# Attention scores from two fp32r parts, two heads on the two halves of the partitions, and row maxima of 2 or 4 heads in one instruction

## The chip, the cores and the metric

The kernel runs on one core of a Trainium2 chip. The metric is the device time of one execution in microseconds (us). Engines: PE multiplies matrices (PEld loads its weights), DVE is VectorE, ACT is ScalarE, POOL is GpSimd, SP issues most of the transfers.

## The reference

One block of a transformer on x of shape (2, 1024, 256), fp32, with 16 heads of 16:

```python
h = _layernorm(x) * (1 + ca) + sa                  # from silu(c) @ wmod
q, k, v = split(h @ W_qkv.T + b_qkv)               # 16 heads of 16
scores = einsum('bnqd,bnkd->bnqk', q, k) * 16 ** -0.5
attn = softmax(where(causal, -inf, scores))        # over keys
x = x + ga * (out @ W_out.T + b_out)
h = _layernorm(x) * (1 + cb) + sb
x = x + gb * ffn(h)      # router over 16 experts (4 groups, top 2; top 4 experts), shared expert
```

The gates and the router's choice of experts need attention's output close to fp32, which is why q and k go through several products.

## The kernel before

**Before attention.** Tokens come in four chunks of 512. For each, DVE makes the statistics (`first_statistics`, L1476), ACT the root, PE turns the rows (`turn`), ACT evicts them as high part and DVE or POOL make the low part, and PE projects q and k in four tiles (`M_ORDER`; L2085) and v (L2107). The bias is added by ACT twice: as fp32 (L1291) and rounded to bf16 (L1294). The tile is then split in three bf16 parts: for chunks 0 and 1 by DVE (`split_tile`: L1540, L1542, L1544), for chunks 2 and 3 by POOL, ACT, POOL (L1063, L1278, L1068). The three parts of q and k are written to DRAM (`qk_parts`, L795) in six rows for each feature, by `Q_PARTS` and `K_PARTS`, so that one product over 6 x 16 = 96 rows gives the sum of six products of parts. `stage` (L797) reads them back, 96 partitions for one group of four heads, in three slots.

**Attention** is a loop over 8 iterations (2 batches x 4 groups of 4 heads). In each, 12 steps (`STEPS`: query half, key tile) have four scores, one for each head (`scores`, L2157; keys x up to 512 queries, causal parts left out). ACT takes the exponential of each out of PSUM (L1377), POOL masks diagonal tiles (L1217), and PE multiplies with the values (`products`, L2140, fp32, a head to each 32 columns of the array). The maximum of each row is taken off inside the product: three more rows of q hold it in three bf16 parts, against ones in k, so that a score is a product over 99 rows. These maxima come from a second set of scores, the units (`score_unit`, L2054; queries x up to 512 keys), which PE makes for iteration n + 1 while it works on n: 48 units for each iteration, one head each, 32 of them with a product that adds the causal mask (L2060). DVE reduces each with one instruction (`row_maximum`, L1511, L1517). `max_parts` (L1605) splits the negated maxima, PE turns them (L2130), `max_copy` brings them to SBUF and `aug` (L725) writes them with three transfers into q's rows 96 to 98.

**Order.** Each engine works its instructions in order. `interleave` (L118) writes PE's order: a score, then as many units as their cost asks for, and after each fourth score the value products of the step before. Units use three banks of PSUM in turn (0 to 2), scores three (3 to 5), products bank 6, the transposes of outputs and maxima bank 7. A score waits for the exponential three before it, a unit for the reduction three before it. In iterations 4 to 6 DVE, PE and ACT also carry pieces of the output projection and of the router (`UNIT_DVE`, `LATE_PE`, `LATE_ACT`); iteration 7 has no units. In chunk 3's projections PE issues 36 of the units of iteration 0 between the other matmuls, 3 (`PER`) at a time, and the last 12 after them. SP's queue holds the writes of parts, the stages, the values and most of the small transfers of the maxima.

**After attention** come the shared expert, the routed blocks of 128 rows (79) and the sums.

## Time and profile before

| | us |
|---|---|
| median of 3 runs | 651.16 (649.86 to 651.72) |
| span of the profiled execution | 644.6 |
| around the span (median less span) | 6.6 |
| before attention | 0 to 89.3 |
| attention, 8 iterations | 89.3 to 369.7 |
| shared expert, routing, sending | 369.7 to 460 |
| routed blocks, sums | 460 to 644.6 |
| busy: PE, DVE, ACT, POOL | 582.1 (90%), 487.5 (76%), 382.8 (59%), 337.9 (52%) |

The execution's own time stands for its span and the 6.6 us around it. Busy times are sums over the whole span; what an engine's saving is worth depends on who is late in each stretch. The ends of matmuls are modelled, so for PE the distance from one start to the next says more than the duration. "fp32r" tiles show as f32 in the rows of matmuls.

### The profile page before, as it was taken

The numbers are of one execution on the slowest core, as the hardware profiler recorded it, in microseconds if no ns is written. First come the engines' busy times: TensorE is split into PE (matmuls) and PEld (weight loads), VectorE is DVE, ScalarE is ACT, GpSimd is POOL, SyncE is SP. The second block draws the span as 40 slices with busy tenths as digits, with TensorE's granted clock in tenths as the row PEclk, the third lists the DMA queues.
The fourth block names the chain that finished last, engine by engine and source line by source line (L and its number), as shares of the span: only waits on it lengthen the run. The fifth ranks groups of instructions, "written<-read, shape, count | busy, mean of one in ns | idle before, by whom it ended". The sixth has DMA issues, their size and how long they took to land. (4 is left out here: it accounts for less than half of the span.)

```text
span 644.6 us, 13664 instructions
## 1 busy us (share of the span) xinstructions
PE 582.1 (90%) x3960; PEld 395.7 (61%) x3960; DVE 487.5 (76%) x1415; ACT 382.8 (59%) x926; POOL 337.9 (52%) x585
## 2 busy tenths in 40 slices
PE   3879879999999999998997799997799999999996
PEld 3657533434343444444342378776799999999985
DVE  4888978888888868776967568898566766666648
ACT  3546437666766656655858552643356777776662
POOL 5524614455747527763738876774144444444430
PEclk9989969999999999998999989999799999999999
DMA  8349965961707273451305243665964444444498
GB/s 270 137 158 288 334 221 151 243 210 71 216 26 224 87 209 141 136 185 63 118 34 174 77 150 115 232 217 207 364 220 134 135 135 134 133 135 134 126 374 335
DMA packets 69066, 113.62 MB, mean 176 GB/s; under 512 B 12578, under 2 KB 51106, under 8 KB 67844
## 3 DMA queue, kind: packets, MB, share of 16 engines
q1 hardware_dynamic: 62036, 93.74, 45.3%
q0 software_dynamic: 6864, 19.01, 7.6%
q8 instruction: 34, 0.56, 0.4%
q14 instruction: 36, 0.29, 0.1%
q10 hardware_dynamic: 96, 0.01, 0.0%
HBM read 60.57 MB, written 49.94 MB: 171 GB/s over the span
## 5 line engine op out<-in xcount | busy, mean ns | idle before, releaser
L1377 ACT ACTIVATE Pr<-bank 128x512 f32<-128x512 f32 (+3 forms) x384 | 165.5, 494 | 94.8 <-PE bank L2166 91.1
L1517 DVE TENSOR_REDUCE mxA<-bank 128x1 f32<-128x128 f32 (+3 forms) x256 | 112.2, 484 | 23.9 <-PE bank L2062 23.7
L1233 POOL DMA_INDIRECT expert_rows<-Y,YIX x79 | 75.7, 959 | 104.0 <-DVE ytmp L1938 75.5
L2166 PE MATMUL bank<-Qs,Ks 99*128 99x512 bf16 (+3 forms) x384 | 118.6, 332 | 8.0 <-ACT Pr L1377 3.8
L2062 PE MATMUL bank<-Ks,Qs 96*128 96x512 bf16 (+3 forms) x384 | 122.1, 334 | 2.2 <-DVE mxA L1517 1.3
L1517 DVE TENSOR_REDUCE mxB<-bank 128x1 f32<-128x512 f32 x128 | 81.5, 681 | 13.5 <-PE bank L2062 13.4
L2152 PE MATMUL bank<-Pr,Vst 128*32 128x512 f32 (+3 forms) x768 | 83.4, 507 | 4.4 <-POOL Pr L1217 4.4
L1167 POOL DMA_INDIRECT chosen_rows<-Hx,pos x64 | 69.9, 1093 | 21.1 <-issue 17.5
L2415 PE MATMUL bank<-W,xh 128*128 x316 | 78.3, 329 | 0.4 <-issue 0.4
L1215 POOL TENSOR_TENSOR tick<-ident 128x1 f32<-128x1 f32 x128 | 25.4, 198 | 100.5 <-ACT Pr L1377 99.7
L2166 PEld LDWEIGHTS bank<-Qs,Ks 99*128 99x128 bf16 x384 | 36.0, 98 | 61.4 <-ACT Pr L1377 38.7
L2060 PE MATMUL bank<-mask,identb 128*128 128x128 bf16 x256 | 55.1, 227 | 7.7 <-DVE mxA L1517 5.3
L1968 DVE TENSOR_TENSOR act_a<-bank,sg 128x176 f32<-128x176 f32 x79 | 27.0, 342 | 45.3 <-ACT sg L1424 45.2
L2062 PEld LDWEIGHTS bank<-Ks,Qs 96*128 96x128 bf16 x384 | 38.1, 99 | 28.8 <-DVE mxA L1517 6.1
L1217 POOL TENSOR_SCALAR_AFFINE_SELECT Pr<-Pr 128x256 f32<-128x256 f32 x128 | 53.3, 416 | 0.0
L2415 PEld LDWEIGHTS bank<-W,xh 128*128 128x128 f32 x316 | 52.3, 189 | 1.3 <-issue 1.0
L2415 PE MATMUL bank<-W,xl 128*128 x158 | 51.3, 325 | 0.0
L1424 ACT ACTIVATE sg<-bank 128x176 f32<-128x176 f32 x79 | 25.1, 317 | 37.4 <-PE bank L2415 37.4
L2060 PEld LDWEIGHTS bank<-mask,identb 128*128 128x128 bf16 x256 | 25.1, 98 | 30.0 <-DVE mxA L1517 13.6
L1439 ACT ACTIVATE Y<-bank 128x256 f32<-128x256 f32 x79 | 30.3, 384 | 13.7 <-PE bank L2444 5.4
L1931 DVE TENSOR_TENSOR xl<-bank,xh 128x256 fp32r<-128x256 f32 x79 | 32.9, 416 | 5.8 <-ACT xh L1418 5.8
L2369 PE MATMUL bank<-ident,G 128*128 128x128 f32 x158 | 30.9, 278 | 6.0 <-DMA G<-chosen_rows 6.0
(254 smaller groups left out, 1314.8 us busy)
## 6 DMA issues: line engine op xcount, KB each, us to landing
G<-chosen_rows SPq DMA_DIRECT2D x79, 132.0 KB
Z<-expert_rows SPq DMA_DIRECT2D x16, 512.0 KB, 12.3
W<-expert_words SPq DMA_DIRECT2D x7, 1088.0 KB, 7.1
qk_parts<-AP SPq DMA_DIRECT2D x16, 384.0 KB, 5.0
Qs<-qk_parts SPq DMA_DIRECT2D x16, 384.0 KB, 4.2
Ks<-qk_parts SPq DMA_DIRECT2D x8, 768.0 KB, 9.0
Wraw<-in_wexp SPq DMA_DIRECT2D x9, 608.0 KB, 5.1
SA<-in_wexp SPq DMA_DIRECT2D x7, 608.0 KB, 10.5
```

The source lines that it names most:

```text
L1167: nc.gpsimd.indirect_dma_start(out=xd, out_offset=bass.IndirectOffsetOnAxis(ap=pos[:, c * TPC + t, j:j + 1], axis=0), in_=chosen(c)[:, t, ...
L1217: nc.gpsimd.affine_select(out=v, in_=v, compare_op=ALU.is_ge, fill=0.0, base=0, pattern=[[0, 2], [1, P]], channel_multiplier=-1).then_inc( ...
L1233: nc.gpsimd.indirect_dma_start(out=zd, out_offset=bass.IndirectOffsetOnAxis(ap=YIX[:, b:b + 1], axis=0), in_=Y[b % YRING], in_offset=None) ...
L1377: nc.scalar.activation(Pr[(2 * s + j // 2) % 4][:, j % 2, 0:w], ebank[p % RING][:, 0:w], ACT.Exp, scale=SCALE).then_inc(exp_done, EXP)
L1517: nc.vector.tensor_reduce(dst, mbank[u % RING][:, 0:w], AX.X, ALU.max).then_inc(m_red, 1)
L1931: nc.vector.tensor_tensor(xl[u % 2][:, :], xbank[:, 0:H], xh[u % 2][:, :].bitcast(F32), ALU.subtract).then_inc(xl_done, 1)
L2060: nc.tensor.matmul(mbank[u % RING][:, w - P:w], identb[:, :], mask[:, :], start=True, stop=False, skip_group_check=True)
L2062: nc.tensor.matmul(mbank[u % RING][:, 0:w], Qs[slot][0:NPR, i // TPC, j, (i % TPC) * P:(i % TPC + 1) * P], Ks[slot][0:NPR, j, k0:k0 + w], ...
L2152: ins = nc.tensor.matmul(pvb[32 * j:32 * j + 32, q0:CH], Vst[slot][:, kt, 32 * j:32 * j + 32], Pr[(2 * s + j // 2) % 4][:, j % 2, 0:w], st ...
L2166: nc.tensor.matmul(ebank[p % RING][:, 0:CH - q0], Ks[slot][0:NAUG, j, kt * P:(kt + 1) * P], Qs[slot][0:NAUG, qc, j, q0:CH], start=True, st ...
L2369: ins = nc.tensor.transpose(xbank[:, k * P:(k + 1) * P], G[u % GRING][:, k * P:(k + 1) * P], ident[:, :])
L2415: ins = nc.tensor.matmul(ubank[u % 2][:, 0:2 * EI], x_part[u % 2][:, k * P:(k + 1) * P], words(u, first + k * 2 * EI, 2 * EI), start=(k == ...
```

## The change

- q and k are split in two parts, kept in fp32 words that TensorE reads as fp32r, and three products of parts (high x high, low x high, high x low) stand in 48 rows in place of six in 96. The splitting: ACT writes the high part (one instruction for chunks 0 and 1, two for 2 and 3), and one DVE or POOL instruction writes the low part; DVE reads the bank itself.
- Two heads stand in one tile, on partitions 0 to 47 and 64 to 111 (`SIDES` = 2, `PAIRS` = 2). The maxima take two rows in place of three, so that a score is a product over 50 rows. `stage` has six transfers in place of three, `aug` four in place of three, writes of a tile two in place of three. Bytes are the same.
- A unit is one or two pairs of heads: 4 heads where 2 pairs x width fit a bank (widths 128 and 256), else 2. It has two banks, one for each side, and one DVE instruction reduces all of it. There are 20 units an iteration, in two slots of two banks (0 to 3). Through the same slots go the transposes of maxima and outputs and the late pieces (up to the last iteration). Scores use banks 4 to 6, products 7.
- The mask is added for each side in two products with 64 rows each, with a table and its copy with swapped halves.
- In chunk 3, 12 units stand between the projections, one (`PER`) at a time.
- The ones in k are written by small transfers in place of POOL's memsets; one zero fill of the block tiles moves to DVE behind attention.

```diff
-Q_PARTS = (0, 1, 2, 0, 1, 0)
-K_PARTS = (0, 0, 0, 1, 1, 2)
+Q_PARTS = (0, 1, 0)
+K_PARTS = (0, 0, 1)
 NPR = len(Q_PARTS) * HD
-NAUG = NPR + 3
+NMAX = 2
+NAUG = NPR + NMAX
+SIDES = 2
+PAIRS = HG // SIDES
+SIDE = P // SIDES
+UNIT_LIST, ROW_FIRST, ROW_COUNT = [], [], []
+for _row in ROWS:
+    _groups = [(0, PAIRS)] if PAIRS * _row[3] <= CH else [(a, 1) for a in range(PAIRS)]
+    ROW_FIRST.append(len(UNIT_LIST))
+    ROW_COUNT.append(len(_groups))
+    UNIT_LIST += [_row + group for group in _groups]
-UNITS = len(ROWS) * HG
+UNITS = len(UNIT_LIST)
...
-    unit_cost = [w + 200 for _, _, _, w in ROWS for _ in range(HG)]
+    unit_cost = [n * SIDES * (w + 100) for _, _, _, w, _, n in UNIT_LIST]
-        while u < UNITS and units * sum(head_cost) < heads * sum(unit_cost):
+        while p % SIDES == SIDES - 1 and u < UNITS and units * sum(head_cost) < heads * sum(unit_cost):
...
-PER = 3
+PER = 1
...
-        mbank, ebank, pvb, tb = allb[0:RING], allb[RING:2 * RING], allb[6], allb[7]
+        mbank = [banks[:, 2 * s:2 * s + 2, :] for s in range(2)]
+        ebank, pvb = allb[4:4 + RING], allb[7]
...
+            for part in range(NMAX):
+                for l in range(SIDES):
+                    row, first = SIDE * l + NPR + part, (part * SIDES + l) * PAIRS * TPC
+                    queue.dma_start(
+                        Qs[slot][row:row + 1, half, :, :].bitcast(F32).rearrange("o a (i q) -> o (a i) q", i=TPC),
+                        MT[half][first:first + PAIRS * TPC, :]
+                    ).then_inc(aug_in[slot][half], 16)
...
-                nc.vector.tensor_tensor(Rq[i % 2][:, :], Fq[m], PT[c % 2][:, 0, m, :], ALU.subtract).then_inc(split_step, 1)
-                dve.wait_ge(split_step, 2 * k + 1)
-                nc.vector.tensor_copy(PT[c % 2][:, 1, m, :], Rq[i % 2][:, :]).then_inc(split_step, 1)
-                dve.wait_ge(split_step, 2 * k + 2)
-                nc.vector.tensor_tensor(PT[c % 2][:, 2, m, :], Rq[i % 2][:, :], PT[c % 2][:, 1, m, :],
-                                        ALU.subtract).then_inc(parts_done[0], 1)
+                tile = PT[k % 8]
+                dve.wait_ge(qk_read, k + 1)
+                nc.vector.scalar_tensor_tensor(out=tile[:, 1, :].bitcast(F32R), in0=qkbank[k % QK_RING], scalar=Bqk[:, m:m + 1],
+                                               in1=tile[:, 0, :], op0=ALU.add, op1=ALU.subtract).then_inc(parts_done[0], 1)
...
-                dst = mxA[:, i, j:j + 1] if diag else mxB[:, i - TPC, j:j + 1]
-                nc.vector.tensor_reduce(dst, mbank[u % RING][:, 0:w], AX.X, ALU.max).then_inc(m_red, 1)
+                dst = (mxA[:, :, i] if diag else mxB[:, :, i - TPC]).rearrange("p (l a) -> p a l", l=SIDES)[:, first:first + pairs]
+                src = mbank[USE[piece][0]][:, :, 0:pairs * w].rearrange("p l (a w) -> p a l w", a=pairs)
+                if pairs == 1:
+                    dst, src = dst[:, 0], src[:, 0]
+                nc.vector.tensor_reduce(dst, src, AX.X, ALU.max).then_inc(read_of(piece), 1)
...
                 if diag:
-                    nc.tensor.matmul(mbank[u % RING][:, w - P:w], identb[:, :], mask[:, :], start=True, stop=False,
-                                     skip_group_check=True)
-                nc.tensor.matmul(mbank[u % RING][:, 0:w], Qs[slot][0:NPR, i // TPC, j, (i % TPC) * P:(i % TPC + 1) * P],
-                                 Ks[slot][0:NPR, j, k0:k0 + w], start=not diag, stop=True,
-                                 skip_group_check=True).then_inc(m_ps, 1)
+                    for part in range(2):
+                        for l in range(SIDES):
+                            rows, k = slice(SIDE * l, SIDE * (l + 1)), P if part == 0 else SIDE
+                            table = (plain, swapped)[part ^ l]
+                            to = bank[:, l, 0:pairs * w].rearrange("p (a w) -> p a w", a=pairs)[:, :, w - k:w]
+                            nc.tensor.matmul(to, table[rows, 0, :],
+                                             table[rows, 1:2, P - k:P].broadcast_to([SIDE, pairs, k]), start=part == 0, stop=False,
+                                             skip_group_check=True)
+                for a in range(first, first + pairs):
+                    for l in range(SIDES):
+                        rows = slice(SIDE * l, SIDE * l + NPR)
+                        ins = nc.tensor.matmul(bank[:, l, (a - first) * w:(a - first + 1) * w],
+                                               Qs[slot][rows, i // TPC, a, (i % TPC) * P:(i % TPC + 1) * P],
+                                               Ks[slot][rows, a, k0:k0 + w], start=not diag, stop=True, skip_group_check=True)
+                ins.then_inc(m_ps, 1)
...
+                a, l = j // SIDES, j % SIDES
+                rows = slice(SIDE * l, SIDE * l + NAUG)
+                nc.tensor.matmul(ebank[p % RING][:, 0:CH - q0], Ks[slot][rows, a, kt * P:(kt + 1) * P],
+                                 Qs[slot][rows, qc, a, q0:CH], start=True, stop=True).then_inc(e_ps, 1)
```

## Rows read from the trace of the kernel before

**Rows 1.** Busy us of each engine (instructions), granted clock, DMA share, GB/s, by stretch
```profile
121.00:152.80 31.80, 31.08 (x238) 12.83 (x235) 27.07 (x64) 21.62 (x50) 18.61 (x48) 1.00 0.63 190
217.20:257.00 39.80, 37.21 (x275) 17.47 (x272) 31.24 (x82) 23.56 (x54) 19.47 (x56) 1.00 0.44 142
335.50:369.70 34.20, 27.73 (x186) 10.78 (x185) 21.24 (x67) 25.52 (x61) 27.95 (x51) 1.00 0.35 118
340.00:360.00 20.00, 16.53 (x115) 6.72 (x115) 13.44 (x45) 15.81 (x35) 16.37 (x26) 1.00 0.49 164
360.00:380.00 20.00, 15.68 (x97) 9.11 (x95) 12.87 (x26) 10.43 (x23) 16.78 (x29) 0.83 0.23 85
```

**Rows 2.** Waits in iteration 1: total us, times, longest
```profile
ACT Pr L1377 <- PE bank L2166: 10.0, 12, 1.3
PEld bank L2166 <- ACT Pr L1377: 4.5, 7, 0.8
DVE mxA L1517 <- PE bank L2062: 1.9, 6, 0.4
```

**Rows 3.** Timeline of PE, a step of iteration 5: start, duration
```profile
273.28 0.38 PE L2062 MATMUL bank<-Ks,Qs 96*128 96x512 bf16 x1
273.59 1.06 PE L2152 MATMUL bank<-Pr,Vst 128*32 128x512 f32 x8
274.58 0.39 PE L2166 MATMUL bank<-Qs,Ks 99*128 99x512 bf16 x1
...
275.42 0.38 PE L2166 MATMUL bank<-Qs,Ks 99*128 99x512 bf16 x1
275.64 0.22 PE L2060 MATMUL bank<-mask,identb 128*128 128x128 bf16 x1
275.70 0.27 PE L2062 MATMUL bank<-Ks,Qs 96*128 96x256 bf16 x1
275.81 0.38 PE L2166 MATMUL bank<-Qs,Ks 99*128 99x512 bf16 x1
```

**Rows 4.** Timeline of PE, the transposes of an output
```profile
286.36 0.66 PE L2137 MATMUL bank<-ident,OT 128*128 128x128 f32 x4
286.86 0.33 PE L2166 MATMUL bank<-Qs,Ks 99*128 99x384 bf16 x1
```

**Rows 5.** Timeline of PE in chunk 2's projections, and two lines' instructions (min/median/max ns)
```profile
54.95 0.39 PE L2085 MATMUL bank<-hh,Wqkh 128*128 128x512 f32 x1
55.18 0.39 PE L2085 MATMUL bank<-hl,Wqkh 128*128 128x512 f32 x1
...
56.11 0.28 PE L2107 MATMUL bank<-Wvh,hl 128*128 128x256 f32 x1
56.23 0.28 PE L2107 MATMUL bank<-Wvl,hh 128*128 128x256 f32 x1
...
L2085 PEld LDWEIGHTS bank<-hl,Wqkh x32: 187/190/334, 18.3 to 69.8; 128*128 128x128 f32 x32
...
L2062 PEld LDWEIGHTS bank<-Ks,Qs x384: 95/98/152, 60.5 to 334.9; 96*128 96x128 bf16 x192
```

**Rows 6.** Timeline of DVE in iteration 1
```profile
130.58 0.20 DVE L1619 TENSOR_SCALAR MP<-mxA 128x16 bf16<-128x16 f32 x1
...
131.37 0.17 DVE L1626 TENSOR_TENSOR MP<-mr,MP 128x16 bf16<-128x16 f32 x1
...
132.09 2.47 DVE L1517 TENSOR_REDUCE mxB<-bank 128x1 f32<-128x512 f32 x4
134.49 0.95 DVE L1517 TENSOR_REDUCE mxA<-bank 128x1 f32<-128x128 f32 x4
```

**Rows 7.** Timelines of DVE, ACT and PE before attention, with idle time and releaser
```profile
30.62 0.68 DVE L1540 TENSOR_TENSOR Rq<-Pr,AP 128x512 f32<-128x512 f32 x1
31.33 0.43 DVE L1542 CAST AP<-Rq 128x512 bf16<-128x512 f32 x1
31.80 0.69 DVE L1544 TENSOR_TENSOR AP<-Rq,AP 128x512 bf16<-128x512 f32 x1
...
40.95 0.21 ACT L1251 ACTIVATE rstd<-rvar 128x4 f32<-128x4 f32 x1 [11.05 <-DVE rvar L1490]
...
42.36 0.80 PE L2085 MATMUL bank<-hh,Wqkh 128*128 128x512 f32 x1 [4.42 <-ACT AP L1294]
```

**Rows 8.** Busy times with DMA share and GB/s, and PE's first score
```profile
75.00:80.00 5.00, 3.82 (x23) 1.89 (x21) 5.00 (x13) 0.00 (x0) 0.43 (x1) 1.00 1.09 383
...
89.32 0.59 PE L2166 MATMUL bank<-Qs,Ks 99*128 99x512 bf16 x1 [3.01 <-DMA Qs<-MT]
```

343 lines of the change are left out of this document (185 added, 158 removed).

## The prediction

> **What bounds the kernel now.** I first read the busy times by stretch [rows 1]. The span of the profiled execution is 644.6 us, and the sum below is made against it. The median of the runs is 651.16 us, 6.6 us more, which lies around the span and which nothing here touches. Attention takes 280 of the 644.6 us, from 89.3 to 369.7. A plain iteration (0 to 3) takes 31.8 us, in which PE is busy for 31.1, DVE 27.1 and ACT 21.6. Iterations 4 to 6, which also carry the output projection and the router, take 38.6 to 39.9 us; 4 is shown. Iteration 7 has no row maxima and takes 34.2 us, with PE at 27.7. Before attention, maxima of iteration 0 are made under the projections and after them.
>
> The waits of iteration 1 [rows 2] say who is late: ACT waits 10.0 us for scores of PE, PE's weight loads wait 4.5 us for ACT, DVE waits 1.9 us. So PE is ahead of nobody: it sets the pace. The busy time of PE is modelled, so I checked it with starts in the timeline [rows 3]. A 512-wide bf16 score takes 0.22 us from start to start, a 256-wide one 0.11, a 128-wide mask product 0.06. The four value products of a step take 0.99 us, in which fp32 needs four passes: 4 x 0.22 = 0.88 for all four heads, so the four column groups already run at the same time. That leaves 0.11 behind them, and the matmul ahead of them takes 0.31 in place of 0.22, so a step pays 0.2 for going to column groups and back.
>
> The sum for PE in a plain iteration: scores 24 x 0.22 + 8 x 0.17 + 8 x 0.11 + 8 x 0.06 = 8.0 us (the widths between by proportion); maxima units the same, 8.0; masks 32 x 0.06 = 1.9; products 9 full-width steps' worth x 0.88 + 12 x 0.20 = 10.3; two transposes of outputs at 0.50 [rows 4] and two of maxima at about 0.2, 1.4. Together 29.6 of 31.8: 2.2 us are stalls. PE is the bound of the loop, and DVE is next.
>
> **Scores and maxima.** Parts fall from six bf16 products over 96 rows to three fp32r ones over 48. Two heads stand on partitions 0 to 63 and 64 to 127, so two successive matmuls use separate halves of the array's rows and write separate banks. No row shows two row halves at once; the column groups of [rows 3] show the like, and I take the same for rows. The price of a single fp32r matmul is in the projections [rows 5]: 512 wide 0.23 us, 256 wide 0.12, each with a weight load of its own that lasts 0.19 against 0.098 in bf16. So one load of fp32r weights passes at least every 0.12 us. I price a pair at 0.24: two loads, with the columns (0.23) under them. The 24 pairs of maxima take 5.8 us and the 24 of scores 5.8, against 8.0 each. Widths under 256 are not shown in fp32r; between 0.06 (bf16) and 0.12 (the load), a pair costs at most the 0.24 that I take, unless the narrow form is much slower.
>
> Masks: each of 12 diagonal units now has four products (two halves of the table on two sides), 48 x 0.06 = 2.9 against 1.9, +1.0. A pair of them could share 0.06, so the lower bound is 1.4. The transposes of maxima and outputs use all rows and stand between products and scores, one more change of shape for each of four, 4 x 0.1 = 0.4. PE's sum becomes 5.8 + 5.8 + 2.9 + 10.3 + 1.4 + 0.4 = 26.6, 3.0 less.
>
> On this the Trainium skill (TensorEngine Tiling, Key Properties) says that changing the tiling mode, not just the tile, drains the engine. The 0.31 and the 0.11 behind 0.88 in [rows 3] agree with it. It also speaks against the change in chunk 3, where 12 units in row halves stand between full-array projections: at 0.1 for each of 24 changes that would be 2.4 us on PE, and with all of it exposed the forecast would be 623 in place of 621.
>
> **DVE.** Four 512-wide reductions in a row take 2.47 us and four 128-wide 0.95 [rows 6]. Less the tail of the last (0.08), that is 0.60 and 0.22 each, so 1.0 ns a column and 0.09 fixed. The columns (18,432 an iteration) stay; 20 instructions do what 48 did, which saves 28 x 0.09 = 2.5 us (0 if reading two banks with one instruction costs as much as it spares). The parts of the maxima lose two of four steps at 0.2 each [rows 6], twice an iteration: 0.8. DVE falls from 27.1 to 23.8 and is not the end: it still has waits for PE's transposes. ACT keeps 21.6. The extra row-maximum buffers are two slots of two banks, which hold 2 x 1.1 us of reductions where three banks held 3 x 0.6, so products of 0.99 are still covered. But maxima and output transposes now pass through the same two slots, and their copies (0.2 and 0.7 us) stand in that ring. With the engines so close I don't let the stalls vanish: 26.6 + 2.2 = 28.8 if all stay, 26.6 if none; DVE's lead grows by 3.3 - 3.0, so its share of the stalls stays and a part of the waits for ACT, whose ring of three now gets scores sooner, goes: I take 28.3. **Saved: 3.5 us** an iteration, in 0 to 3: 14. In 4 to 6 the same scores and units pass under the same PE bound (37.2 busy of 39.8 in 4), 3.5 x 3 = 10.5. In 7 no units run and ACT's own work and waits fill it: 0.
>
> **Before attention.** In the first chunk DVE splits four tiles at 1.8 us each (three instructions) [rows 7]; behind them in its queue stand the statistics of chunk 3, for which ACT waits 11.05 us, and ACT's queue holds the evictions for which PE waits 4.42. One instruction of 0.69 at most replaces the three: 4 x 1.15 = 4.6 us, all on that chain. The second chunk's split lies beside a dense PE. From 73 us on DVE's maxima bound; they save another 2.5 + 0.8 once. Against it stand the transfers: [rows 8] has the DMA engines full at 383 GB/s, and the first score at 89.32 waits 3.01 us for the rows of maxima that had to pass them. The bytes are the same (six of 2 against three of 4), so this stage ends no sooner than its start was moved. SP has eight small transfers more ahead of the first write, at a time in which it is idle (its last load is issued at 11 us, the first write at 25.7). ACT's four small issues in place of three (+0.6) lie under the last reductions. I take 5.5, between 4 and 7. Behind attention only banks and one memset move: 0.
>
> **The sum.** 651.2 - 14 - 10.5 - 5.5 = 621.2, predicted **621** (span about 614.6).
>
> **The rivals.**
> The row halves do not overlap (the change doesn't do what it says). Each fp32r matmul then costs 0.23, 0.175, 0.12 and 0.12: 17.7 for both kinds against 16.0, masks 3.3 against 1.9, transposes +0.1, so +3.2 an iteration: 651.2 + 7 x 3.2 - 5.5 + 1 = **669**, slower. The place is every pair of scores and units; it decides where less than about half of the overlap comes, since 29.6 lies midway between 26.6 and 32.8. The column groups speak against it, and the missing row for it.
> They overlap in part. At 0.30 a pair in place of 0.24, 48 pairs cost 2.9 more; where 512 wide only, 24 x 0.06 = 1.4 an iteration, 10 in all: **631**. The Trainium skill (TensorE: Matmul & The Clock Gate, Measured speedup vs the span model) has four row tiles at 3.07 times; an estimate by it is 77% of the ideal, which gives this 0.30.
> PE's lighter load lets its clock fall. From 340 to 360 us it is granted 1.00 with PE busy for 16.5 of 20, from 360 to 380 only 0.83 with 15.7 [rows 1]. At 1.2 GHz for a tenth of the loop, 2.6 us an iteration: **639**. It was at 1.00 through all plain iterations, and steps leave no long idle piece.
> Both relieved fully: two halves load weights at the same time, masks pair at 1.4, and stalls shrink as queues are looser: PE 24, DVE 23.8, an iteration of 26: 651.2 - 7 x 5.8 - 7 = **604**.
>
> **How the numbers follow.** Forecast 0.55, full relief 0.08, partial 0.14, clock 0.05, no overlap 0.13; 0.05 is left for what I don't see, 0.03 of it near no change and 0.01 on either side. A measurement of this kernel tells 0.3% from no change. Faster is 0.55 + 0.08 + 0.14 + 0.05 + 0.01 = 0.83, same 0.03, slower 0.14. The likeliest's own range is 612 to 630 (unknown stalls of 1 us an iteration either way). The range 603 to 650 leaves out no overlap and half of full relief, under 2 in 10.
>
> **What would show it.** In the timeline two scores or two units of different sides start within 0.05 us of each other where both banks are free; apart by 0.23, the last rival holds. A plain iteration takes about 28.3 us, with ACT's wait for PE well under 10 us. A four-head reduction of 256 wide takes 1.1 to 1.2 us. Iteration 7 stays at 34. ACT's wait for the statistics falls from 11 to about 6 us, and the first score starts near 84. The prediction is wrong if the two slots make PE wait for DVE, if narrow fp32r matmuls are far slower than their loads, or if the sharing of slots by the transposes holds back the maxima.

## The result, and the profile after

The changed kernel takes 708.25 us (median of 4, 704.25 to 710.82) against 650.51 us for the kernel before on the same chip (649.14 to 651.72): a ratio of 1.088, 95% interval 1.084 to 1.092. Here and below, times are medians of a kernel's fast runs (within 1.5% of its fastest), and the profiles of e1 and e5 are of slower runs. It is 58 us slower where 30 us faster were forecast. The profiled execution took 709.61 us with a span of 706.9, against a span of 644.6.

The page after, cut to the busy line and TensorE's granted clock in 40 slices of 17.7 us:

```profile
PE 629.8 (89%) x4088; PEld 432.5 (61%) x4088; DVE 460.1 (65%) x1144; ACT 373.3 (53%) x910; POOL 324.5 (46%) x565
...
PEclk9999658995699659989669578999979999999999
```

DVE and ACT are no busier than before (487.5 and 382.8 us there), PE is, by 48 us, though its parts fell from six to three. The digits 5 and 6 in the clock line say that in a good part of attention PE had its lower clock, 1.2 GHz (0.50).

The same in stretches: the first is attention from 76 us to the last copy of outputs (L1364), the second what lies behind; the third and fourth are two passes through the same steps, from the copy of one half of outputs to the next, at either clock. Columns are busy us and instructions of each engine, granted clock, DMA share, GB/s.

```profile
76.00:433.90 357.90, 315.93 (x2061) 152.27 (x2062) 216.60 (x355) 183.09 (x423) 170.61 (x410) 0.78 0.41 119
433.90:706.90 273.00, 255.72 (x1704) 236.10 (x1704) 193.48 (x678) 159.54 (x439) 129.25 (x130) 0.97 0.57 194
...
128.10:138.50 10.40, 9.21 (x85) 4.77 (x85) 8.25 (x13) 6.37 (x18) 6.74 (x17) 1.00 0.53 121
167.70:183.90 16.20, 15.69 (x85) 8.01 (x85) 8.18 (x12) 6.69 (x17) 9.03 (x20) 0.50 0.46 88
```

The same view of the kernel before, the matching stretches:

```profile
76.00:373.90 297.90, 271.58 (x1950) 116.52 (x1949) 235.08 (x596) 184.03 (x422) 169.11 (x411) 0.97 0.46 146
373.90:644.60 270.70, 253.65 (x1704) 234.84 (x1704) 193.16 (x677) 159.31 (x439) 129.25 (x130) 0.98 0.57 195
...
124.36:133.64 9.28, 9.18 (x74) 4.09 (x73) 7.86 (x19) 6.40 (x18) 5.70 (x16) 1.00 0.58 133
124.36:156.16 31.80, 31.07 (x235) 12.83 (x234) 27.07 (x64) 21.61 (x52) 18.61 (x46) 1.00 0.52 154
```

(The third row is this half of an iteration, the fourth a whole iteration.)

Since the clock has two levels, a mean of 0.78 over 357.9 us means 2 x 0.22 x 357.9 = 157 us at 1.2 GHz; before, 0.03 x 2 x 297.9 = 18 us. (The mean has two decimals, so such a figure is good to some 4 us.) The same 85 products take 16.2 us at the low clock and 10.4 at the high one, so each microsecond at the low clock loses 5.8 / 16.2 = 0.36. By that rate, an estimate from one pair of stretches, **the clock costs (157 - 18) x 0.36 = 50 us.** The span grew by 62.3 us. The first score comes 3.3 us earlier, what lies behind attention takes 2.3 us more, so attention from its first score grew by 63.3, and 13 us of this remain. At the high clock too the changed kernel is the slower one, 10.4 against 9.3 us in this half of an iteration. Two pauses add 5.8 us: PE waits 2.86 us at 155.69 and 2.94 us at 235.50 for GpSimd's masks, and in the kernel before no wait of this kind is over 1 us until 371 us. Two different things failed, then: a large one, the clock, and a saving that isn't there at either clock.

The waits from 100 to 400 us, to be set beside [rows 2] (which are for one iteration):

```profile
ACT Pr L1435 <- PE bank L2245: 139.7, 84, 5.2
...
DVE mxA L1578 <- PE bank L2126: 67.0, 49, 6.0
PEld bank L2245 <- ACT Pr L1435: 57.5, 99, 1.7
```

Everyone waits for PE's products, and PE's loads wait for ACT; no wait for DVE's slots or the turned maxima is among the large ones.

The timeline of a pair of scores and a pair of maxima at the full clock answers to [rows 3]:

```profile
215.11 0.66 PE L2213 MATMUL bank<-ident,OT 128*128 128x128 f32 x4
215.69 0.50 PE L2245 MATMUL bank<-Qs,Ks 50*128 50x512 f32 x2
216.03 0.39 PE L2126 MATMUL bank<-Ks,Qs 48*128 48x512 f32 x2
216.26 0.39 PE L2245 MATMUL bank<-Qs,Ks 50*128 50x512 f32 x1
216.92 0.49 PE L2245 MATMUL bank<-Qs,Ks 50*128 50x512 f32 x1 [0.28 <-ACT Pr L1435]
```

Two halves start as one (x2), so they do overlap. But the pair at 215.69 is followed only 0.34 us later, the next pair 0.23 us later. The first stands behind transposes over all rows, with no wait of PE before it. Then one score of the next pair starts alone, since the bank of the other isn't free yet (it waits 0.28 us for ACT): the halves are out of step.

The reductions over two banks in the groups by shape:

```profile
L1578 DVE TENSOR_REDUCE mxB<-bank 128x2 f32<-128x1024 f32 x64 | 78.2, 1223 | 29.5 <-PE bank L2126 28.5
```

PE's timeline has the first score, as in [rows 8]:

```profile
86.00 0.80 PE L2245 MATMUL bank<-Qs,Ks 50*128 50x512 f32 x2 [2.25 <-DMA Qs<-MT]
```

### The profile page after: what moved, and what is told of

Same layout as the page of the kernel before. It is cut to its first block and busy times, and to the rows that moved or that the text cites. A ratio compares the mean times of both kernels' runs of the same rounds, so it can differ in the third digit from the quotient of the medians.

```text
span 706.9 us, 13625 instructions
## 1 busy us (share of the span) xinstructions
PE 629.8 (89%) x4088; PEld 432.5 (61%) x4088; DVE 460.1 (65%) x1144; ACT 373.3 (53%) x910; POOL 324.5 (46%) x565
## 5 line engine op out<-in xcount | busy, mean ns | idle before, releaser
L1578 DVE TENSOR_REDUCE mxA<-bank 128x4 f32<-128x512 f32 (+2 forms) x96 | 99.3, 1046 | 76.4 <-PE bank L2126 75.6
L2245 PE MATMUL bank<-Qs,Ks 50*128 50x512 f32 (+3 forms) x384 | 126.0, 492 | 22.2 <-ACT Pr L1435 18.8
L2245 PEld LDWEIGHTS bank<-Qs,Ks 50*128 50x128 f32 x384 | 60.5, 223 | 101.2 <-ACT Pr L1435 68.3
L2229 PE MATMUL bank<-Pr,Vst 128*32 128x512 f32 (+3 forms) x768 | 102.8, 616 | 8.5 <-POOL Pr L1284 8.5
L2126 PE MATMUL bank<-Ks,Qs 48*128 48x512 f32 (+3 forms) x384 | 104.6, 470 | 3.0 <-DVE mxA L1578 1.0
L1578 DVE TENSOR_REDUCE mxB<-bank 128x2 f32<-128x1024 f32 x64 | 78.2, 1223 | 29.5 <-PE bank L2126 28.5
L2126 PEld LDWEIGHTS bank<-Ks,Qs 48*128 48x128 f32 x384 | 55.5, 235 | 8.1 <-DVE mxA L1578 2.3
L2120 PE MATMUL bank<-plain 64*128 64x128 bf16 (+1 forms) x192 | 38.8, 255 | 7.5 <-DVE X L1705 1.9
L2229 PEld LDWEIGHTS bank<-Pr,Vst 128*32 128x32 f32 x768 | 16.6, 119 | 36.1 <-issue 14.4
L2120 PE MATMUL bank<-swapped 64*128 64x128 bf16 (+2 forms) x192 | 38.2, 257 | 0.0
L1982 DVE TENSOR_TENSOR xl<-bank,xh 128x256 fp32r<-128x256 f32 x79 | 32.8, 415 | 6.1 <-ACT xh L1476 6.0
```

The source lines that it names most:

```text
L1578: nc.vector.tensor_reduce(dst, src, AX.X, ALU.max).then_inc(read_of(piece), 1)
L1982: nc.vector.tensor_tensor(xl[u % 2][:, :], xbank[:, 0:H], xh[u % 2][:, :].bitcast(F32), ALU.subtract).then_inc(xl_done, 1)
L2120: nc.tensor.matmul(to, table[rows, 0, :], table[rows, 1:2, P - k:P].broadcast_to([SIDE, pairs, k]), start=part == 0, stop=False, skip_grou ...
L2126: ins = nc.tensor.matmul(bank[:, l, (a - first) * w:(a - first + 1) * w], Qs[slot][rows, i // TPC, a, (i % TPC) * P:(i % TPC + 1) * P], Ks ...
L2229: ins = nc.tensor.matmul(pvb[32 * j:32 * j + 32, q0:CH], Vst[slot][:, kt, 32 * j:32 * j + 32], Pr[(2 * s + j // 2) % 4][:, j % 2, 0:w], st ...
L2245: nc.tensor.matmul(ebank[p % RING][:, 0:CH - q0], Ks[slot][rows, a, kt * P:(kt + 1) * P], Qs[slot][rows, qc, a, q0:CH], start=True, stop=T ...
```

## The experiments

Thirteen kernels. Times of the kernel before are from the same chip and occasion. "Low" is the time at 1.2 GHz between 76 us and the last copy of outputs, worked out from the stretch's mean clock as above.

**Is a stacked pair as cheap as thought?** Two kernels of TensorE series alone: all series run warm, then again behind a pause of about 11 us, with full-array bf16 products after each. Core of the first:

```python
S1 = [("halves","r",50,512), ("halves","b",50,512), ("halves","r",64,512), ("full","b",99,512),
      ("full","r",99,512), ("one","r",50,512), ("full","b",50,512)]   # halves: rows 0.. and 64.. in turn
```

> A kernel of its own: it computes nothing of the reference (the input is copied to the output) and issues 512-wide matmuls on random data in series: fp32r on 50 rows of alternate halves, bf16 on 50 rows of alternate halves, fp32r on 64 rows of alternate halves, bf16 on 99 rows, fp32r on 99 rows, fp32r on 50 rows of one half, bf16 on 50 rows alone; each series runs 96 or 72 matmuls, pauses about 10 us, runs as many again, and full-array bf16 stands between series. Each matmul has its own weights. Theory A, the fp32r weight load holds up the pair: a pair of halves costs 0.34 us in fp32r and about 0.22 in bf16. Theory B, row halves overlap only partly: 0.34 in both types. Theory C, the clock does not come back on half-used rows: after the pause the 50-row series stay at granted 0.50 to their end (over 20 us), while the 99-row ones are back at 1.00 within 7 us. Rival D, pauses alone set the clock: all series come back within 7 us.

> The same kernel of its own with narrow matmuls: fp32r on 50 rows of alternate halves 256 and 128 wide, bf16 on 64 rows of alternate halves 128 wide, fp32r on 99 rows 128 wide, fp32r on 128 rows 256 wide. If the load of fp32r weights sets the pace, 256 and 128 wide cost the same in halves, 0.12 us a matmul or more. If narrow fp32r is slow in itself, the 128-wide one on 99 rows takes over 0.12 us. Clock: by theory C the series in halves stay at 0.50 after the pause, by rival D they come back.

The fp32r halves of 50 rows in turn, then (behind "...") the same product on one half only, each in a stretch without a pause:

```profile
48.50:59.30 10.80, 10.80 (x97) 9.18 (x96) 0.00 (x0) 0.00 (x0) 1.00 0.00 0
...
334.00:364.00 30.00, 30.00 (x71) 23.02 (x72) 0.00 (x0) 0.00 (x0) 0.50 0.00 0
```

In the second: halves of 256 columns, of 128, of 128 again behind a pause, and one product of 99 rows and 128 columns after another, at first and later:

```profile
49.30:55.00 5.70, 5.70 (x95) 5.70 (x96) 0.00 (x0) 0.00 (x0) 1.00 0.00 0
85.10:90.40 5.30, 5.30 (x97) 5.30 (x96) 0.00 (x0) 0.00 (x0) 1.00 0.00 0
103.00:111.00 8.00, 8.00 (x78) 8.00 (x78) 0.00 (x0) 0.00 (x0) 0.50 0.01 2
...
153.80:160.40 6.60, 6.60 (x61) 6.57 (x59) 0.00 (x0) 0.00 (x0) 1.00 0.01 2
180.00:199.00 19.00, 19.00 (x91) 19.00 (x91) 0.00 (x0) 0.00 (x0) 0.50 0.00 1
```

In a stream a pair costs 0.23 us for 512 columns (10.8 / 97 is 0.11 a product), so neither the loads nor a partial overlap hold it up: both theories fall. At the full clock 256 columns cost 0.06 us a half and 128 hardly less, 0.055 (96 products in 5.3 us); alone, 99 rows of 128 columns cost 0.11. Of the clock, neither theory C nor rival D holds as it stood. Halves in turn, 512 wide, kept 1.00 and had it back in their second series behind the pause, against theory C. But one half alone fell to 0.50 in the middle of its first series, with no pause before, and sat there with PE busy all the time, 0.42 us a product, and so did 99 rows of fp32r 128 wide; halves 128 wide ran at 0.50 behind the pause to the end of their series. That speaks against rival D.

**Few rows inside the kernel.** The kernel before, with three of its six bf16 products left out (51 and 48 rows, one head after the other):

```diff
-Q_PARTS = (0, 1, 2, 0, 1, 0)
-K_PARTS = (0, 0, 0, 1, 1, 2)
+Q_PARTS = (0, 1, 0)
+K_PARTS = (0, 0, 1)
```

> The kernel before with three bf16 products of two parts in place of six of three: products over 48 and 51 rows, one head after the other, nothing stacked, all else as before; the third part of q and k and the products with it are left out of the scores. Theory C, few rows in use keep the clock down: PE's work is the same in columns, but the clock stays at 0.50 for long pieces of attention and the time is above 680 us. Rival D, the pauses and the stacking do it: the clock is as before, and the time is 640 to 651 us, since a third of the written rows is gone from the start.

835.97 us in the fastest run (three others took 853.03 to 857.58) against 659.31 (656.5 to 663.22), 27% slower, with as many products of the same widths, and less data. Its attention, in the run of 853.03:

```profile
76.00:573.40 497.40, 484.28 (x1967) 149.11 (x1967) 257.24 (x601) 199.19 (x423) 172.17 (x413) 0.57 0.23 70
```

2 x 0.43 x 497.4 = 428 us low, of 497. Beside the rows in use only the bytes of staging and a few early writes changed, so this shows the mechanism in the kernel itself: with half the rows in each product and the same number and widths of products, the clock was low for 86% of this stretch.

**More rows, pairs in step, fillers.** Four edits of the changed kernel.

```diff
 e2: scores over both halves (zeros in the unused rows between)
-                rows = slice(SIDE * l, SIDE * l + NAUG)
+                rows = slice(0, SIDE + NAUG)
 e3: one wait for a pair
-                if n or p >= RING:
-                    pe.wait_ge(exp_done, n * (EXP * HEADS) + EXP * (p - RING + 1))
+                if p % SIDES == 0 and (n or p + 1 >= RING):
+                    pe.wait_ge(exp_done, n * (EXP * HEADS) + EXP * (p + 1 - RING + 1))
 e4: a product of all rows ahead of each unit of maxima; e5: e3 and e4
+                nc.tensor.matmul(bank[:, 0, 0:4 * P]..., identb, plain[:, 1:2, :].broadcast_to([P, 4, P]),
+                                 start=True, stop=True, skip_group_check=True)
```

> The changed kernel, with each score product run over rows 0 to 113 of its two tiles, so over both halves at once, in place of its own 50 rows; rows 32 to 63 are set to 0 in the beginning so that the unused ones add nothing. What it computes is the sum of the two stacked heads' scores for either of them: each head's own scores are left out. The number and width of the products stay the same, but two of them can no longer run beside each other. Clock theory (products that use half of the array's rows let the clock fall, and keep it at 1.2 GHz): the 50-row products are now those of the row maxima alone, the scores at 229 ns each keep the clock up for most of the attention; the low stretches, some 165 us up to 440, shrink to under 80, mean granted clock 0.93 or more, and the time falls by 30 to 60 us, to 650 to 680. Out-of-step theory (the pair of halves doesn't overlap because its second score waits for an exponential, and the halves lag): there was little overlap to lose, and none is won: 700 to 725, the clock as it was at 0.88.

> The changed kernel with one wait moved: the first score of a stacked pair waits until the banks of both are free, and the second for nothing, so that the two issue together and run beside each other. Nothing is left out. Out-of-step theory: a pair at full clock goes from 0.34 to 0.24 us (512 wide); 24 pairs an iteration, some 1.5 to 2.5 us of each of 8 iterations, and as the PE has to wait less at a low clock also a few more: 680 to 695. Clock theory: the pair is shorter and the engine idles more, still with half of the rows, so the low stretches stay (160 us or more up to 440) or grow, and the time stays within 1% of 708 or goes up.

> The changed kernel with one product over 128 rows and 512 columns (bf16, constant tables) in front of each unit of the row maxima, into the unit's own bank, which the unit then starts anew. Nothing is left out. It adds 160 products of 0.216 us at full clock: 34.6 us of TensorE time, 4.3 an iteration. Clock theory: products of all rows between those of half the rows keep the clock up or bring it back; the low stretches shrink to under 80 us up to 440 and the time falls by 10 to 40 us in spite of the added work, to 670 to 700. Out-of-step theory: only work is added, on an engine that was busy 89%: 730 to 745. If the clock follows pauses alone (rows have no part), it is the same as the latter at 0.88.

> Both edits of the two kernels before this one together: pairs of scores in step, and a product of all rows in front of each unit. Nothing is left out. Clock theory with full overlap: 34.6 us of added products, 20 us saved by pairs, the clock at 1.00 for most of the attention: 640 to 675. Out-of-step theory alone: the fillers' 35 us against 20 saved: 715 to 725. Neither: as the one with fillers alone.

Against 649.52 us (647.07 to 651.92) before: e2 711.93 (706.72 to 714.22), ratio 1.095; e3 697.3 (693.31 and 701.31), 1.074; e4 728.5 (727.26 and 729.74), 1.122; e5 726.4 (721.78 and 731.06), 1.120. e3 to e5 have two runs each. Attention in e2, e3 and e4, and in e2 a whole iteration at full clock:

```profile
76.00:436.00 360.00, 329.48 (x2111) 156.77 (x2110) 224.89 (x365) 187.83 (x425) 176.28 (x413) 0.85 0.43 128
...
178.09:212.23 34.14, 33.19 (x251) 15.34 (x252) 24.65 (x32) 21.76 (x51) 18.78 (x46) 1.00 0.44 115
```

```profile
76.00:428.60 352.60, 296.65 (x2061) 131.14 (x2062) 217.31 (x355) 186.82 (x423) 172.03 (x410) 0.78 0.41 121
```

```profile
76.00:452.00 376.00, 346.47 (x2217) 148.90 (x2216) 222.08 (x359) 185.06 (x423) 170.82 (x410) 0.86 0.38 112
```

Low time: 157 us in the changed kernel, 108 in e2, 155 in e3, 105 in e4. Rows do lift the clock, as the clock theory says, but its forecasts of the time missed. In e2, 49 us less at the low clock are worth 18 us by the rate above. Its zeros are written first, so that its first copy of outputs comes 9 us later than in the changed kernel (112.4 us against 103.2); from there to the last copy it takes 323.6 us against 330.7, 7 us less, and running the scores one after the other ate the rest. In e4, 52 us less at the low clock are worth 19 us, the fillers are 35 us of work, and the time is 20 us above the changed kernel's. What I expected of e2 and e4 took the clock for the whole loss. e5 missed the 640 to 675 us of the clock theory too. Its time is 2 us under e4's, which is nothing, given the spread, so it is as the one with fillers alone; its profile is of a run of 743.89 us and isn't compared.

Out-of-step, the rival, missed as well: e3 lies between the two forecasts for it, some 10 us under the changed kernel. e3 did put the pairs in step and took 19 us off PE's busy time in attention. But halves of an iteration with the same clock in both kernels got no shorter: 10.7 us against 10.4 at full clock, and 16.2 and 18.2 us at 0.50 in either. The gain stands in one place. From the copy of outputs at 218 or 219 us to the one two halves later, e3 takes 37.2 us and the changed kernel 46.9, because one of the pauses for GpSimd is missing and only 7 us are low there in place of 27. The half at full clock says why pairs in step save nothing, e3 here, the changed kernel above:

```profile
129.20:139.90 10.70, 8.79 (x87) 4.25 (x85) 8.43 (x12) 6.52 (x19) 6.87 (x17) 1.00 0.61 136
```

PE is busy 0.4 us less and the half takes 0.3 us longer. With three banks for scores, a pair must wait until the exponential before the last is done, and ACT then waits for the pair: PE idles 1.9 us and ACT 4.2 of 10.7. I read this as both in turn being the path, so that PE's sum alone no longer sets it; no run has a longer ring to show it.

**All rows, and the pauses.** e7 takes e2 further: the maxima too run over both halves (rows 0 to 111), with the lower half's two rows of maxima put out of the way. e6 moves two splits on GpSimd.

```diff
 e7, beside the edits of e2
-                        rows = slice(SIDE * l, SIDE * l + NPR)
+                        rows = slice(0, SIDE + NPR)
 e6
-PRE_POOL = {(1, 7): [11], (2, 7): [12], (3, 5): [13], ...}
+PRE_POOL = {(1, 11): [11], (2, 11): [12], (3, 5): [13], ...}
```

> The kernel of the run with all rows in the scores, with the products for the row maxima run over both halves too (rows 0 to 111), so that no product of queries and keys is left that uses one half alone. To keep the two rows with the maxima out of those, the lower half's two lie in rows 114 and 115, which no product reads, and the scores read those of the upper half. It computes the sum of the two stacked heads for both, with the upper one's maxima: each head's own scores and maxima are left out. The number, type and width of the products stay as in the changed kernel. Clock theory in its plain form (what lets the clock fall is that only half the rows are in use): the low stretches, 159 us of the attention in the changed kernel and 108 in the run with the scores alone, fall to under 40 us (18 in the kernel before), and the time to 660 to 680, what is left over the kernel before being the type (229 against 216 ns, 8 iterations of some 34.2 against 32 us at full clock). If the type or the narrow products (114 ns for 128 columns in either layout) are what counts, 80 us or more stay low and the time is 695 to 720.

> The changed kernel with the first two splits of expert weights on GpSimd moved from behind step 7 to behind step 11 of their iterations, so that no masking of a diagonal tile stands behind their wait for a DMA in the same iteration. Nothing is left out. Two of the low stretches (155.9 to 190.0 and 234.4 to 261.7) began behind pauses of 2.9 us in which TensorE waited for that masking. If pauses make the clock fall: both stretches go or shrink to under 10 us, 15 to 25 us less: 683 to 693. If the work of half the rows does, and the pause only set the moment: they begin elsewhere, the low total stays at 140 us or more, and the time within 8 us of 706.

e7: 708.95 us (707.88 to 718.14, which is the profiled run), ratio 1.089 (1.086 to 1.092). e6: 704.28 (699.46 to 704.39), ratio 1.079 (1.073 to 1.084), both against 650.52. e7's attention, a half of an iteration and a whole one at full clock:

```profile
76.00:440.90 364.90, 337.78 (x2110) 177.41 (x2109) 225.12 (x365) 185.75 (x424) 174.82 (x413) 0.91 0.42 126
...
225.20:236.90 11.70, 11.22 (x84) 5.95 (x84) 8.00 (x12) 6.45 (x17) 7.07 (x31) 1.00 0.32 78
199.50:236.90 37.40, 36.44 (x251) 18.71 (x252) 24.75 (x32) 21.59 (x50) 17.41 (x60) 1.00 0.30 89
```

e7 has 66 us low, so with all rows the clock is most of the way back (18 before); its forecasts were under 40 us low and 660 to 680 us, or 80 and more and 695 to 720, so only the second's time came. Its time is no better, since its first copy of outputs comes 9 us later, as in e2, and since without overlap the half takes 11.7 us at the full clock, 1.3 more than in the changed kernel and 2.4 more than before. The new set of products, run one after the other, is dearer than the old one by far more than the 0.229 to 0.216 a product that had been expected (34.2 us an iteration expected, 37.4 measured, 31.8 before), and I had that wrong.

The whole iterations also tell what overlap is worth. Between scores and maxima e7 has none (37.40 us), e2 has it in the maxima alone (34.14), and e9 below, whose short half takes 10.4 us as in the changed kernel, has it in both (32.35). So the maxima's overlap gives 3.3 us an iteration and the scores' 1.8.

In e6 the two low stretches began elsewhere and the low total stayed (156 us, from a mean of 0.78 over 353.8 us): the two pauses of 2.9 us, of which this is one, in the timeline of PE in the changed kernel, set at most the moment of a fall. They cost their own length: from the first copy of outputs to the last, e6 takes 325.1 us against 330.7.

```profile
155.69 0.94 PE L2229 MATMUL bank<-Pr,Vst 128*32 128x512 f32 x4 [2.86 <-POOL Pr L1284]
```

**What fp32r costs behind a wait.** Groups of 512-wide products with a wait for one small copy on ACT after each group:

```python
S3 = [("halves","r",50,512,16,28), ("full","r",99,512,8,28), ("halves","r",50,512,8,45), ("full","r",99,512,4,45),
      ("full","b",99,512,4,45), ("halves","b",50,512,8,45), ("full","b",99,512,2,60), ("halves","b",50,512,4,60)]
```

> A kernel of its own, with no part of the computation: TensorE does groups of products, 512 columns each, and waits after each group for one copy of 128 elements on ScalarE, some 0.5 to 0.6 us; eight series of some 50 us, each behind 48 products of all rows back to back. In order: fp32r halves of 50 rows in turn, 16 a group (1.84 us at full clock); fp32r 99 rows, 8 a group (the same time); fp32r halves, 8 a group (0.92 us); fp32r 99 rows, 4; bf16 99 rows, 4; bf16 halves, 8; bf16 99 rows, 2; bf16 halves, 4. Clock theory: where TensorE pauses a third of the time, the halves fall to 1.2 GHz, with twice the time a group, while 99 rows of the same columns stay at 2.4 GHz; the halves without pauses were at full clock, so the rows in use count only together with the pauses. If only pauses count, halves and 99 rows fall, or don't, alike in groups of the same time. Rivals on the overlap of halves have no part in it: 0.115 us a half at full clock in either case.

The last six series, in order:

```profile
210.00:260.00 50.00, 37.49 (x252) 21.09 (x252) 9.58 (x31) 0.00 (x0) 1.00 0.00 1
290.00:340.00 50.00, 37.26 (x126) 20.89 (x125) 9.89 (x32) 0.00 (x0) 1.00 0.00 0
370.00:420.00 50.00, 36.08 (x140) 10.81 (x140) 10.73 (x35) 0.00 (x0) 1.00 0.00 0
450.00:500.00 50.00, 36.13 (x280) 10.70 (x276) 10.54 (x35) 0.00 (x0) 1.00 0.00 1
530.00:590.00 60.00, 43.16 (x85) 5.38 (x84) 12.98 (x42) 0.00 (x0) 0.50 0.00 0
620.00:690.00 70.00, 50.20 (x196) 6.52 (x196) 15.14 (x49) 0.00 (x0) 0.50 0.00 1
```

Eight halves take the time of four products of 99 rows (31.5 groups in 50 us, 1.59 us a group, in either), so overlap is whole here as well, and the clock doesn't tell them apart: my clock theory in the form "halves fall when there are pauses" is refuted. Halves that do overlap are as good for the clock as full rows; both kinds were at 0.50 with half as many products between waits (the last two rows). The surprise is the third row: bf16 has 35 groups, 1.43 us. Of the 0.16 us a group that fp32r takes more, 4 x 0.013 = 0.05 is its longer products, and 0.106 is left, once a group. In the changed kernel a pair of 384 columns whose loads waited for ACT shows the like:

```profile
127.88 0.19 PEld L2245 LDWEIGHTS bank<-Qs,Ks 50*128 50x128 f32 x2 [0.20 <-ACT Pr L1435]
```

The next product starts 0.34 us later, where 384 columns in a row would take some 0.17 by proportion; a part of this may be the change of type, since the next is a bf16 mask. The pair at 215.69 above shows as much more (0.34 in place of 0.23) with no wait but a change from all rows to halves before it, so a wait isn't the only thing that brings this price.

```python
("r waits", 64), ("b waits", 64), ("half waits", 96), ("2b 2r", 128), ("2b 2b", 128), ("2r 2r", 128), ("blocks of 8", 192)
```

> A kernel of its own, with no part of the computation: seven series of products on TensorE, 512 columns each unless said, behind 24 products of all rows. In the run of groups, the first fp32r product behind a pause kept the engine 0.335 us until the next, 0.106 more than one in a row, and the weight load behind it began 0.10 us late, for 50 and for 99 rows alike; with bf16 it was 0.22 and nothing late. Here no wait ever stops anything: it is for a semaphore that has long been reached. Series: (1) fp32r 99 rows with such a wait ahead of every second product; (2) the same in bf16; (3) fp32r halves of 50 rows in turn with a wait ahead of every second; (4) two bf16 products of 128 columns and two fp32r of 512 in turn, 99 rows; (5) the same in bf16 alone; (6) the same in fp32r alone; (7) fp32r halves, eight products on one half and then eight on the other. Theory W (the weight load after a wait comes late in fp32r, whether the wait stops or not): (1) 282 ns a product in place of 229, (2) 216, (3) 141 in place of 115. Theory S (only a true stop does it): 229, 216, 115. Of a change of type: if the first fp32r product behind bf16 ones pays the same, a group of four takes 0.1 us more in (4) than its parts, 0.11 and 0.46; if not, (4) is 0.57 us a group. Clock theory (the part of the array in use counts, over time, and not that both halves come up): in (7) the clock falls as it did with one half alone, to 0.50; if it is enough that both halves are used in turn, it stays at 1.00.

The first three series, the one with types in turn, and the last:

```profile
31.00:44.00 13.00, 13.00 (x59) 10.75 (x58) 0.00 (x0) 0.00 (x0) 1.00 0.00 1
51.00:63.00 12.00, 12.00 (x57) 5.42 (x56) 0.00 (x0) 0.00 (x0) 1.00 0.01 1
70.00:80.00 10.00, 10.00 (x92) 8.23 (x90) 0.00 (x0) 0.00 (x0) 1.00 0.01 2
86.00:106.00 20.00, 20.00 (x127) 11.62 (x126) 0.00 (x0) 0.00 (x0) 1.00 0.00 1
162.00:187.00 25.00, 25.00 (x191) 22.59 (x190) 0.00 (x0) 0.00 (x0) 1.00 0.01 1
```

A wait that stops nothing costs nothing: some 0.22 us a product in the first row and 0.21 in the second (a few at the edges are counted in), 0.11 for halves. Theory S holds, only a true stop costs. A group of two bf16 and two fp32r products takes 4 x 20 / 127 = 0.63 us, where two bf16 of 128 columns (0.11) and two fp32r (0.46) add to 0.57: 0.06 for going to the other type and back, if each of the 12 diagonal units an iteration pays it, 0.7 us, an estimate. The last series missed its aim: even eight products on one half and eight on the other ran at 0.13 us each, largely beside each other, so it says nothing of one half at a time.

**Rows alone.** One product after the other, four a group (then eight of 256 or 128 columns, then 16 of bf16), the same waits; and the score products of the changed kernel over 64 rows, 14 of them zeros:

```diff
 e9, beside the writing of zeros
-                rows = slice(SIDE * l, SIDE * l + NAUG)
+                rows = slice(SIDE * l, SIDE * (l + 1))
```

> A kernel of its own, as the one with groups and one pause after each (some 0.6 to 0.8 us), with one product after the other and no overlap: groups of 4 products of 512 columns in fp32r over 99, 80, 64 and 50 rows, then in bf16 over 64 and 50 rows, then fp32r over 99 rows with 8 products of 256 columns and with 8 of 128, then bf16 over 99 rows with 16 of 128. Durations and pauses are the same over the first six, only the rows change. Rows by themselves: 99 stays at 1.00 as before, 50 falls to 0.50, the change lies at 80 or 64. Overlap and shapes alone: all of the first six stay at 1.00. Narrow fp32r shapes: 8 products of 128 (0.91 us at 114 ns) fall where 16 of 128 in bf16 (some 0.9 us) stay; by pauses and busy time alone, both are as the first.

> The changed kernel with the score products run over all 64 rows of their half, 14 of them set to 0 in both tiles in the beginning, in place of 50. Nothing is left out and no product gets longer; first scores come some us later, as the zeros are written first (112.4 against 103.2 us for the first copy of outputs where half as many were written). If the number of rows that a product uses counts for the clock by itself, rows of zeros too: the low stretches of the attention shrink from 159 us to 90 to 130, and the time is 690 to 705 in spite of the later start. If only rows with data count, or overlap and shapes alone: 140 to 170 us low and 708 to 718.

The series of m5: fp32r over 99, 80, 64 and 50 rows, bf16 over 64 and 50, then fp32r 256 and 128 wide and bf16 128 wide over 99 rows:

```profile
45.00:80.00 35.00, 26.24 (x89) 14.72 (x88) 6.80 (x22) 0.00 (x0) 1.00 0.00 0
100.00:160.00 60.00, 50.18 (x97) 28.25 (x98) 7.61 (x25) 0.00 (x0) 0.50 0.00 0
190.00:245.00 55.00, 46.23 (x91) 25.67 (x89) 6.81 (x22) 0.00 (x0) 0.50 0.00 0
270.00:330.00 60.00, 50.33 (x98) 28.17 (x99) 7.47 (x25) 0.00 (x0) 0.50 0.00 0
355.00:405.00 50.00, 41.47 (x88) 9.37 (x88) 6.55 (x22) 0.00 (x0) 0.50 0.00 0
435.00:485.00 50.00, 41.19 (x89) 9.37 (x88) 6.80 (x22) 0.00 (x0) 0.50 0.00 0
505.00:545.00 40.00, 30.04 (x200) 24.97 (x198) 7.72 (x25) 0.00 (x0) 1.00 0.00 0
570.00:625.00 55.00, 45.81 (x187) 41.49 (x187) 7.11 (x23) 0.00 (x0) 0.50 0.00 1
645.00:680.00 35.00, 25.60 (x384) 21.50 (x384) 7.23 (x24) 0.00 (x0) 1.00 0.00 1
```

This settles it outside the kernel: with the same columns, type and waits, the product over 99 rows kept 1.00 and those over 80, 64 and 50 ran at 0.50; and at 99 rows, fp32r 128 wide ran at 0.50 where bf16 of that width, and fp32r of twice the width, kept 1.00. (bf16 over 99 rows, 512 wide, kept 1.00 in m3.) In the kernel e9 took 707.04 us (703.75 to 708.26), ratio 1.085 (1.077 to 1.092) against 651.27. Its attention, and a whole iteration at full clock:

```profile
76.00:428.30 352.30, 311.32 (x2109) 150.93 (x2108) 223.72 (x364) 183.34 (x424) 179.17 (x415) 0.81 0.44 130
...
176.05:208.40 32.35, 29.59 (x252) 13.98 (x252) 24.74 (x32) 20.93 (x51) 18.74 (x46) 1.00 0.45 121
```

2 x 0.19 x 352.3 = 134 us low against 157, for 14 rows of zeros that cost no product any time. Its first copy of outputs comes at 112.8 us, 9.6 later than in the changed kernel, since GpSimd writes the zeros first; from there to the last copy it takes 315.5 us against 330.7. The late start ate the gain. The rows did not give all of these 15 us: 23 us less at the low clock are worth 8 by the rate above, and the two pauses of 2.9 us for GpSimd are missing in e9. Beside e6, which lacks them too, it is 134 us low against 156. Both numbers lie between what e9's two forecasts said (90 to 130 us low and 690 to 705 us; 140 to 170 and 708 to 718), and it is one profile, so in the kernel this is a hint that rows of zeros count; m5 shows the rows by themselves.

The iteration of 32.35 us is the only whole one with both overlaps and the full clock: 0.55 us more than before, where 3.5 less had been forecast.

No experiment came near the kernel before, so no version that beats both was found.

## Why the prediction was wrong

- **The clock (rival at 0.05, sized at a tenth of the loop and slowed to 639): the step that failed most.** 157 us at 1.2 GHz, 44% of the time from 76 us to the last copy of outputs, cost 50 us by the rate of the two equal stretches. I argued that the clock was at 1.00 in all plain iterations and that no long idle piece was left. But the change halves the rows that a product uses while PE's time hardly falls. PE busy for 15.7 of 16.2 us at 0.50 shows that "busy" was the wrong thing to look at. Rows as a cause are shown by e1 in the kernel before and by m5 alone; that they are the bulk of the low time in the changed kernel is likely by e2 and e7 (157, 108, 66 us as rows are added), but these two also end the overlap, so the rows are not the only thing that changed in them.
- **A pair of halves at 0.24 us.** Right in a stream (0.23), wrong in the kernel. There, a pair behind a wait or behind a change of shape takes some 0.1 us more, and at other places the two halves are out of step. The 0.106 us behind each wait was in no row of before that I read as such; the fp32r projections of [rows 5] run without waits. The overlap itself mostly came: by the sum it was to give 32.8 - 26.6 = 6.2 us an iteration, some 3.1 for each kind, and it gave 3.3 for the maxima and 1.8 for the scores.
- **The saving of 3.5 us an iteration (28.3 us): the second step that failed.** At the full clock an iteration takes 32.35 us, 0.55 more than before. Of the 4.05 us between, 1.2 are overlap that didn't come. The largest part is the price without overlap: e7 takes 37.4 us where the sum of the rival "no overlap" gives 31.8 + 3.2 = 35.0, 2.4 too little. The rest, 0.45, stays open. It isn't the narrow products: a pair of 128 columns takes 0.11 us in a stream, and the sum had 0.24 for every pair of any width (the rival's had 0.12 a product, where 0.11 was measured). The price behind waits and changes of shape, 0.106 us each, would make 2.4 us with 23 such places an iteration, an estimate that nobody counted out. And the bound was not PE's sum: when e3 took 19 us off it, the halves of an iteration with the same clock in both kernels got no shorter.
- **Masks +1.0, changes of shape +0.4.** The two were not measured by themselves in the kernel. By m4 they leave out changes of type, some 0.7 us.
- **DVE: 28 x 0.09 = 2.5 us saved.** An instruction over two banks (1024 elements) takes 1.223 us, and four single ones took 2.47 [rows 6]: 2 x 1.22 = 2.45. The fixed part saved is next to nothing at that width. DVE's busy time did fall by 27 us over the kernel, and nothing came of it, as DVE was not late: from 100 to 400 us it waits 67 us for PE ahead of one kind of reduction alone.
- **Before attention, 5.5 us.** 3.3 came: the first score at 86.00 in place of 89.32. ACT's wait for the statistics did not fall (11.12 us in place of 11.05); it ends at 38.88 in place of 40.95, since DVE, done sooner with its splits, now stood 3.5 us waiting for PE. The transfer of the maxima's rows still holds the first score, for 2.25 us.
- **Iteration 7 at no change, behind attention 0.** Behind it 2.3 us more. Iteration 7 also ran partly at the low clock: from the copy of outputs at 390.3 to the last at 433.9, it takes 43.6 us against 35.2 before (338.7 to 373.9).
- **The rival "no overlap", 669.** Its mechanism was wrong, since the overlap is there. e7, which is nearly that case at the full clock, shows it also priced too low: 5.6 us more an iteration than before, where it had 3.2.

What stays open: how the low time of the changed kernel divides between rows, narrow fp32r products and halves out of step. In e7 all rows are in use and 66 us are still low, against 18 before; narrow fp32r can be the reason by m5, but no kernel changed the widths alone. Nor is the price behind waits and changes of shape counted in the kernel. Wider reductions alone, without the new products, weren't tried either.

## What to carry to other kernels

A change that makes each product of TensorE smaller, but not its time, can cost the clock: before halving the rows of products, run a short series of the new ones with the loop's waits and look at the granted clock, not at the busy time. Price a product in the company that it will have, behind a wait and beside its neighbours' types, not in a stream. And when two engines wait for each other through a short ring, the sum of one of them need not be the bound: in e3, 19 us less work on PE made none of the stretches at equal clock shorter.

## What the runs showed of the hardware

- In groups of four 512-wide products with the same wait, those over 99 rows kept 2.4 GHz (fp32r in m5, both types in m3), and those over 80, 64 and 50 rows in fp32r and over 64 and 50 in bf16 ran at 1.2. One half alone fell to 1.2 GHz in the middle of a series and stayed there with no pause inside its next one (71 products in 30 us). So a high busy share doesn't say that the clock is high.
- fp32r behind a true wait takes 0.106 us more than in a row (1.59 against 1.43 us for a group of four, less 0.05 for the type); a wait already met costs nothing (0.22 us a product).
- Row halves overlap whole in fp32r and bf16 (m3): eight of 50 rows in the time of four of 99. Even with eight in a row on one half they took 0.13 us each (191 in 25 us, m4), where one half alone takes 0.22 at the same clock (27 products from 297 to 303 us in m1).
- fp32r hardly gets shorter below 256 columns: a half in a pair takes 0.06 us at 256 and 0.055 at 128, and 99 rows alone 0.11 at 128 against 0.12 at 256 in [rows 5].
